# The last pair's second half of values moved into the tail of each batch, with a turning DMA of its own

## The reference

```
x = x + attention(layernorm(x))        16 heads of 64, causal, w_qkv 1024 x 3072, w_out 1024 x 1024
x = x + cross(layernorm(x), ctx)       query/key of ctx (1024 x 512 by 512 x 128), softmax over 1024 x 1024,
                                       the normed x times the attention's transpose
x = x + gated_ffn(layernorm(x))        8 experts, low rank 8, the best expert chosen per token
```

## Time and profile before

| | |
|---|---|
| Time, median of 3 runs | 2646.89 us (2642.32 to 2650.19) |
| The profiled execution | 2647.89 us |
| Its span in the trace | 2646.1 us |
| PE busy | 2395.5 us, 91% of the span |
| DVE, ACT, POOL busy | 69%, 31%, 27% |
| Chain that ended last | PE 59%, DVE 19%, DMA 8%, issue 7% |

### The profile page before, as it was taken

The page is one execution under the profiler, slowest core; times in us unless marked ns, Lnnn a source line. Parts: engine busy times, 40 slices in busy tenths (PEclk is TensorE's granted clock), DMA queues, the critical chain, the costliest instruction groups (busy, mean ns, idle before and its releaser), DMA issues.

```text
span 2646.1 us, 38038 instructions
## 1 busy us (share of the span) xinstructions
PE 2395.5 (91%) x14411; PEld 1175.0 (44%) x14411; DVE 1817.5 (69%) x3457; ACT 816.8 (31%) x1629; POOL 714.9 (27%) x981
## 2 busy tenths in 40 slices
PE   4888998799989999899998999979988999988996
PEld 1334443454544444454453444444444444445444
DVE  6677887657856777656866777765695767675566
ACT  2444333322123333321213333341221333342110
POOL 3332444124202222213412222212430222221220
PEclk9999999899989999999998999989998999999997
DMA  7687888866537767866745777686662676776543
GB/s 213 158 207 167 190 182 176 208 145 148 126 93 151 146 136 148 181 160 149 153 104 124 142 149 141 131 200 158 142 145 86 137 149 143 144 167 163 112 86 90
DMA packets 983131, 393.50 MB, mean 149 GB/s; under 512 B 936796, under 2 KB 946012, under 8 KB 982948
## 3 DMA queue, kind: packets, MB, share of 16 engines
q1 hardware_dynamic: 980356, 381.63, 65.9%
q10 hardware_dynamic: 2592, 9.44, 1.1%
HBM read 122.56 MB, written 33.55 MB: 59 GB/s over the span
## 4 chain that ended last, share of the span: by engine, by line
PE 59%; DVE 19%; DMA 8%; issue 7%; ACT 3%; POOL 3%; SPq 1%; ACTq 0%; POOLq 0%; DVEq 0%
PE ps_p L564 8%; PE ps_p L566 8%; PE ps_p L565 8%; DMA r<-pn 7%; PE ps_s L564 7%; PE ps_s L566 6%; PE ps_s L565 6%; PE ps_s L624 6%; PE ps_o L651 5%; DVE pn L885 5%; DVE peak L925 2%; ACT probs L803 2%; DVE bn L890 2%; PE ps_s L629 1%; POOL pn L1180 1%
## 5 line engine op out<-in xcount | busy, mean ns | idle before, releaser
L1180 POOL TENSOR_SCALAR pn<-probs,rden 128x640 f16<-128x640 f32 (+7 forms) x512 | 396.4, 787 | 1264.4 <-DVE rden L937 760.7
L803 ACT ACTIVATE probs<-ps_s,low,sizes 128x640 f32<-128x640 f32 (+7 forms) x512 | 421.2, 826 | 861.2 <-DVE low L928 750.9
L885 DVE SCALAR_TENSOR_TENSOR pn<-probs,rden,pn 128x640 f16<-128x640 f32 (+7 forms) x512 | 461.3, 937 | 153.9 <-POOL pn L1180 152.4
L564 PE MATMUL ps_p<-r,w 128*128 128x512 f16 x1344 | 515.7, 384 | 3.4 <-DVE qk L885 3.2
L565 PE MATMUL ps_p<-r,w 128*128 128x512 f16 x1344 | 515.1, 383 | 0.0
L566 PE MATMUL ps_p<-r,w 128*128 128x512 f16 x1344 | 514.8, 383 | 0.0
L624 PE MATMUL ps_s<-qk 64*128 64x512 f16 (+3 forms) x2304 | 243.3, 338 | 122.3 <-ACT probs L803 111.7
L925 DVE TENSOR_REDUCE peak<-ps_s 128x2 f32<-128x1280 f32 (+3 forms) x128 | 241.5, 1887 | 89.5 <-PE ps_s L629 86.5
L651 PE MATMUL ps_o<-r,vn 128*64 128x512 f16 (+3 forms) x2304 | 214.1, 343 | 35.4 <-issue 35.2
L624 PEld LDWEIGHTS ps_s<-qk 64*128 64x128 f16 x2304 | 91.6, 96 | 268.9 <-ACT probs L803 146.5
L566 PEld LDWEIGHTS ps_p<-r,w 128*128 128x128 f16 x1344 | 132.5, 99 | 162.2 <-issue 6.1
(11 more groups left out here) (191 smaller groups left out, 3523.5 us busy)
## 6 DMA issues: line engine op xcount, KB each, us to landing
w<-w_pairs SPq DMA_DIRECT2D x72, 512.0 KB, 4.0
r<-wo_pairs SPq DMA_DIRECT2D x16, 1024.0 KB, 6.2
w_raw<-in_x SPq DMA_DIRECT2D x32, 512.0 KB, 4.3
out<-r SPq DMA_DIRECT2D x32, 512.0 KB, 2.9
w_pairs<-w SPq DMA_DIRECT2D x24, 512.0 KB, 7.0
qk<-in_x SPq DMA_DIRECT2D x24, 512.0 KB, 4.5
w_raw<-in_ctx_t SPq DMA_DIRECT2D x16, 512.0 KB, 5.2
w_raw<-in_w_qkv ACTq DMA_DIRECT2D x12, 512.0 KB, 6.3
```

Of the source, the lines that this page charges most:

```text
L564: pe.matmul(ps, lh, rh, start=start and k == ks[0], stop=False)
L803: act.activation(probs_part(q, j, w), ps_s[:, j, scores(q)], ACT.Exp, bias=low[:, n % 2, i:i + 1], scale=sc(n), accum_out=den[:, n % 2, i: ...
L885: dve.scalar_tensor_tensor(out=to, in0=bank, scalar=scale, in1=rounded, op0=ALU.mult, op1=ALU.subtract).then_inc(ok, 1)
L1180: pool.tensor_scalar(to, src, scale, 1.0, ALU.mult, ALU.mult).then_inc(ok, 1)
```

## The change

The four parts P210 to P213 leave the body of pair 6 of each batch and stand in the tail, two ahead of S2 and two ahead of S3. CH21 and CL21 move later in the ACT and DVE lists. `vt16` and `vn` are laid out by halves of the tokens; the last pair's values are turned by two DMAs, V for the first half at the old place in the SP list and V1 after T3. SP's tail opens with T0, and OI0 to OI3 stand behind it. OI0 to OI2 wait only until the part of P21 that reads the same rows is over; KI, KH and KL each wait for their own third of the projections; M0 of the last pair waits for the first half of the values alone.

```
 PE_TAIL
-    S2 S3 M1- S4 G0 S5 G1 M0 S6 G2 B00 S7 ...
+    P210 P211 S2 P212 P213 S3 M1- S4 G0 S5 G1 M0 S6 G2 B00 S7 ...
 DVE_TAIL
-    X0 L70- L71- CL21 R0 X1 L00 L01 X2 R1 L10 ...
+    X0 L70- L71- R0 X1 L00 L01 X2 R1 CL21 L10 ...
 ACT_TAIL
-    E00 E01 CH21 E10 E11 E20 E21 KH JH0 ...
+    E00 E01 E10 E11 E20 E21 CH21 KH JH0 ...
 SP_TAIL
-    OI0 OI1 T0 T1 OI2 T2 OI3 JI2 T3 T4 JI3 T5 ...
+    T0 OI0 OI1 T1 OI2 OI3 T2 JI2 T3 V1 T4 JI3 T5 ...
...
-        vt16 = sb(es, "vt16", [P, 2, SEQ], F16)
-        vn = sb(es, "vn", [P, 2, 2, TB, P], F16)
+        vt16 = sb(es, "vt16", [P, 2, 2, HALF], F16)
+        vn = sb(es, "vn", [P, 2, 2, 2, PARTS, P], F16)
...
+        xt_free = sem("xt_free")
...
+                    if p == PAIRS - 2 and off == 1 and kind == "P" and args[:2] == (2, 1):
+                        continue
...
                     elif kind == "V":
+                        if n % PAIRS < PAIRS - 1:
+                            sp.wait_ge(c_ok, 6 * n + 6)
+                            if n >= 2:
+                                sp.wait_ge(m_ok, 2 * n - 2)
+                            sp.dma_start_transpose(vn[:, n % 2, :, :, :, :].rearrange("p h s k d -> p (h s k) d"),
+                                                   vt16[:, :, :, :].rearrange("p h s d -> p (h s d)")).then_inc(v_in, 16)
+                        else:
+                            h = len(a)
+                            sp.wait_ge(c_ok, 6 * n + 5 + h)
                             sp.wait_ge(m_ok, 2 * n - 2)
+                            sp.dma_start_transpose(vn[:, n % 2, h, :, :, :].rearrange("p s k d -> p (s k) d"),
+                                                   vt16[:, h, :, :].rearrange("p s d -> p (s d)")).then_inc(v_in, 16)
...
                     elif kind == "OI":
-                        sp.wait_ge(part_ok, 6 * PAIRS * (b + 1))
+                        if i < PARTS - 1:
+                            sp.wait_ge(xt_free, 3 * b + i + 1)
+                        else:
+                            sp.wait_ge(part_ok, 6 * PAIRS * (b + 1))
...
                     elif kind == "KI":
-                        sp.wait_ge(part_ok, 6 * PAIRS * (b + 1))
+                        sp.wait_ge(part_ok, 6 * PAIRS * (b + 1) - 4)
...
                         if part == PARTS - 1:
                             mm.then_inc(part_ok, 1)
+                        elif p == PAIRS - 1 and (t, h) == (2, 1):
+                            mm.then_inc(xt_free, 1)
...
-                        pe.wait_ge(v_in, 16 * (n + 1))
+                        pe.wait_ge(v_in, 16 * (n + 1 + b + (g if p == PAIRS - 1 else 0)))
...
                     elif kind == "KH":
                         act.wait_ge(k_in, 16 * (b + 1))
+                        act.wait_ge(part_ok, 6 * PAIRS * (b + 1) - 2)
...
                     elif kind == "KL":
                         dve.wait_ge(kh_ok, b + 1)
+                        dve.wait_ge(part_ok, 6 * PAIRS * (b + 1))
```

More of the change, by code:

```diff
@@ L61 @@
 PE_TAIL = """
-    S2 S3 M1- S4 G0 S5 G1 M0 S6 G2 B00 S7 G3 B01 B10 B11 M1 B20 N0 B21 N1 B30 N2 B31 N3 B40 N4 B41 N5 B50 N6 B51 N7
+    P210 P211 S2 P212 P213 S3 M1- S4 G0 S5 G1 M0 S6 G2 B00 S7 G3 B01 B10 B11 M1 B20 N0 B21 N1 B30 N2 B31 N3 B40 N4 B41 N5 B50 N6 B51 N7
     B60 B61 B70 B71 Z00 Z01 Z10 Z11 Z20 Z21 F0 Z30 Z31 F1 D0 Z40 Z41 F2 D1 U0 Z50 Z51 F3 D2 U1 Z60 Z61 F4 D3 U2
@@ L67 @@
 DVE_TAIL = """
-    X0 L70- L71- CL21 R0 X1 L00 L01 X2 R1 L10 L11 R2 X3 KL JL0 R3 OL1- X4 L20 L21 QL0 JL1 R4 L30 L31 X5 L40
+    X0 L70- L71- R0 X1 L00 L01 X2 R1 CL21 L10 L11 R2 X3 KL JL0 R3 OL1- X4 L20 L21 QL0 JL1 R4 L30 L31 X5 L40
     L41 QL1 JL2 R5 OL0 X6 L50 L51 R6 QL2 JL3 X7 L60 L61 R7 QL3 RA0 L70 L71 RA1 LB0 OL1 CX0 LL0 LB1 CR0 RA2 CX1 CLO0
@@ L77 @@
 ACT_TAIL = """
-    E00 E01 CH21 E10 E11 E20 E21 KH JH0 E30 E31 OH1- QH0 JH1 E40 E41 E50 E51 QH1 JH2 OH0 E60 E61 QH2 JH3 E70 E71
+    E00 E01 E10 E11 E20 E21 CH21 KH JH0 E30 E31 OH1- QH0 JH1 E40 E41 E50 E51 QH1 JH2 OH0 E60 E61 QH2 JH3 E70 E71
     QH3 LX0 OH1 CE0 LX1 CE1 CE2 CE3 LX2 CE4 CE5 CE6 CE7 AX0+ AX1+ AX2+ TX0 LX3 AX3+ TX1
@@ L89 @@
 SP_TAIL = """
-    OI0 OI1 T0 T1 OI2 T2 OI3 JI2 T3 T4 JI3 T5 RI0 T6 RI1 T7 WD0+ WD1+ WD2+ RI2 RI3 CT0 LT0 CT1 RI4
+    T0 OI0 OI1 T1 OI2 OI3 T2 JI2 T3 V1 T4 JI3 T5 RI0 T6 RI1 T7 WD0+ WD1+ WD2+ RI2 RI3 CT0 LT0 CT1 RI4
     LT1 RI5 CT2 CT3 RI6 CT4 CT5 RI7 CT6 CT7 AI0+ AI1+ AI2+ AT0+ AT1+ AI3+ LT2 AT2+
@@ L208, in decoder_layer @@
         c_probs = qk16[1][:, :].bitcast(F32).rearrange("p (s d) -> p s d", s=2)
-        vt16 = sb(es, "vt16", [P, 2, SEQ], F16)
-        vn = sb(es, "vn", [P, 2, 2, TB, P], F16)
-        xh3 = vn[:, 1, :, :, :].rearrange("p s k d -> p s (k d)")
+        vt16 = sb(es, "vt16", [P, 2, 2, HALF], F16)
+        vn = sb(es, "vn", [P, 2, 2, 2, PARTS, P], F16)
+        xh3 = vn[:, 1, :, :, :, :].rearrange("p h s k d -> p h (s k d)")
         probs0 = sb(es, "probs0", [P, 2 * SEQ])
@@ L456, in attend @@
                     elif kind == "V":
-                        sp.wait_ge(c_ok, 6 * n + 6)
-                        if n >= 2:
+                        if n % PAIRS < PAIRS - 1:
[7 more added lines that the diff above has]
+                            sp.wait_ge(c_ok, 6 * n + 5 + h)
                             sp.wait_ge(m_ok, 2 * n - 2)
-                        sp.dma_start_transpose(vn[:, n % 2, :, :, :].rearrange("p s k d -> p (s k) d"),
-                                               vt16[:, :, :].rearrange("p s d -> p (s d)")).then_inc(v_in, 16)
+                            sp.dma_start_transpose(vn[:, n % 2, h, :, :, :].rearrange("p s k d -> p (s k) d"),
+                                                   vt16[:, h, :, :].rearrange("p s d -> p (s d)")).then_inc(v_in, 16)
                 def constants():
@@ L650, in attend @@
                                 for j in range(2):
-                                    mm = pe.matmul(ps_o[rows(j), g, c:HALF], vn[:, n % 2, vs, kb, rows(j)],
+                                    mm = pe.matmul(ps_o[rows(j), g, c:HALF], vn[:, n % 2, kb // PARTS, vs, kb % PARTS, rows(j)],
                                                    keys_of(g, j, s, kb), start=kb == 0 and vs == 0 and s == 0,
@@ L774, in attend @@
                             if n > 0:
-                                act.wait_ge(v_in, 16 * n)
-                            to = vt16[:, 0, half(h)]
+                                act.wait_ge(v_in, 16 * (n + n // PAIRS))
+                            to = vt16[:, h, 0, :]
                         act.activation(to, proj_bank(n, t, h), ACT.Copy, scale=Q_OUT).then_inc(ch_ok, 1)
@@ L913, in attend @@
                         else:
-                            hi, lo = (vt16[:, s, half(h)] for s in range(2))
+                            hi, lo = (vt16[:, h, s, :] for s in range(2))
                         pair_rest(lo, proj_bank(n, t, h), Q_OUT, hi, c_ok)
```

## The result

The changed kernel takes 2651.89 us (median of 7 runs, 2648.05 to 2654.91) against 2645.27 for the kernel before (7 runs, 2641.78 to 2650.19): ratio 1.0026, 95% interval 1.0016 to 1.0036. It is slower, by 4 to 10 us; the forecast was 14. The way was right and the size twice too large. The measured time lies in the forecast's range, 2650 to 2676, only because its lower end had been put there for the warm M1-; on its own the forecast had 2655 to 2676.

A forecast was written before the change was run, and what follows sets the result against it. PE, busy nine tenths of the span, was the bound, with T7's and T3's landings setting the tails. Head - 2.6, gap + 13.8 and clock + 3.0 made + 14.2 us on 2646.9: 2661 us, range 2650 to 2676.

The forecast's parts named there:

- warm M1-: Rival: denser PE work in the head brings M1- to full clock, 8.6 us gained, 2652 us; chance 0.12.
- The order of SP: Tails: T0 holds SP until M1- ends, all four OI loads then precede T3, so M0 starts later; 13.8 us lost.
- the gap: From M1-'s end to M0's start, over four tails: forecast 86.4 us against 72.6 before, 13.8 us lost.
- E: The end of M1- in a tail; forecast T1's landing near E + 10 and M0 at E + 21.6.
- small gaps: Allowance of 0.5 us per tail added to the byte sum up to T3's landing, giving M0 at E + 21.6.
- M1- left as it is: M1- in the tails keeps its time, since it still waits 3 to 4 us and the clock falls there; 0.
- The clock at M0: M0 and S6 run slow in all four tails after a hole of about 7 us; 3.0 us lost.
- The head: Ahead of M1-: X0, L71 and T7's issue come 0.6 us earlier, KI moves out of T7's way; 2.6 us gained.
- Hidden loads: Rival: transposes pass beside loads or faster than 208 GB/s, M0 stays, only the head counts; 2644 us, chance 0.07.
- loads and transposes pass at one rate: The page's rate in the DMA queue, counted inside the hidden-loads rival; chance 0.03 of its 0.07.
- PE work decides: Rival: PE's own work bounds the tail, so 5.2 us of projections are saved in each, 20.8 us; 2626, chance 0.05.
- Stalls: Rival: T1 and T2 behind loads each lose up to 1.9 us, 15 us more, 2676; with the forecast, chance 0.74.

The follow-up runs named there:

- e2: The kernel before with SP's new order alone (T0 ahead of OI0 and OI1, OI2 and OI3 behind T1): 2662.88 us, ratio 1.0054.
- e4: The kernel before with OI3 moved behind T3 and JI2 behind T2, projections and values as before: 2630.22 us, ratio 0.9941.
- e5: The kernel before with 8 useless matmuls behind S3, inside the wait ahead of M1-: ratio 1.0.
- e10: The kernel before with SP's new order and 8 useless matmuls ahead of M1-: ratio 1.0032.
- e7: The changed kernel with OI0, OI1 ahead of T0, OI3 behind T3, 8 useless matmuls ahead of M1- and 14 between G0 and S5: 2624.89 us, 0.9916.
- e9: The changed kernel with OI0, OI1 ahead of T0, OI3 behind T2, and one V for the last pair instead of two: ratio 1.0005.
- e6: The changed kernel, its SP order too, with 8 useless matmuls ahead of M1- and 20 ahead of M0: 2652.23 us, ratio 1.0015.
- e1: The changed kernel with OI0 and OI1 ahead of T0 again and OI3 behind T2: 2640.26 us, ratio 0.997.
- e3: The changed kernel with OI0 and OI1 ahead of T0, JI2 behind T2 and OI3 behind T3: 2627.43 us, ratio 0.9928.

## Why the prediction was right in its way and wrong in its size

**The order of SP.** Right, and the largest term. Forecast + 13.8 us for the gap, measured + 11.3 in the changed kernel and + 10.4 in e2. T1's landing (E + 10.8 for E + 10), the idle DMA engines during M1- and M0 on T3's landing came as written. The size is too large by the 0.5 us that I added to each tail for small gaps: without it the sum gives M0 at E + 21.1, and the four tails measured 21.8, 20.6, 21.1 and 20.4, on average 21.0. In the second tail the DMA engines are busy for 0.97 of the time from M1- to M0, so there are few gaps to pay for; in the kernel before T2 and T3 were issued only as L2 and L3 ended (1121.54 and 1126.68 us), which is where its gaps may lie.

**M1- left as it is.** This is the term that failed. The prediction took it at 0, with a rival of 8.6 us at a chance of 0.12; it measured - 5.4 us (26.2 to 20.8). The step behind the 0 was that the clock falls in the wait of 3 to 4 us just ahead of M1-, which the change leaves there. Two things in it were wrong. The waits of before weren't all of that length: the earlier trace rows have 1.94, 4.02, 3.44 and 2.73 us, and M1- took 7.12 us behind the shortest. And the clock hadn't fallen in the wait. PE in the two waits of tails one and two, the kernel before first (the third number from the end is the granted clock):

```profile
469.50:471.40 1.90, 0.01 (x1) 0.50 1.06 240
1105.60:1109.50 3.90, 0.00 (x0) 0.50 1.18 179
```

```profile
471.75:474.00 2.25, 0.00 (x0) 1.00 1.08 232
1104.60:1108.60 4.00, 0.01 (x1) 0.96 1.19 243
```

Before, the clock was at 0.50 through the whole wait: it had gone by then, with S3, behind the hole of 3.50 us. In the changed kernel PE is dense from S0 to S3 and the clock stands at 1.00 and 0.96 in the same wait. So in tail one M1- runs at full rate from its start; in tail two it starts at 0.50 and is back at 1.00 from 1112 us on, half way (5.92 us). So what loses the clock ahead of M1- is the hole ahead of S3, which the moved projections fill. That they do it, the table shows (0 of 12 tails with M1- at 4.41 us in before, e2 and e4, 13 of 20 with them moved). e5 and e10 show that useless matmuls bring the clock back too, if not always: M1- took 4.41 to 4.86 us in their eight tails, and in e7, with the same fill on top of the moved projections, 5.98 in one of four.

What it is worth depends on the order: nothing in the old one (e5, e9); in the new, most of it by the changed kernel against e2 (M1- 5.3 us less, gap 0.9 more), about half by e10 against e2 (M1- 8.5 us less, tails 4.5 less). So it mattered here because the same edit that made the loads wait for M1- made its length count. How much of it comes through isn't settled, as e6 shows. The rival's time, 2652 us, is near what was measured, but in part by luck: M1- gave 5.4 us and not 8.6, and the gap cost 2.5 less than forecast.

**The clock at M0.** Forecast + 3.0 for M0 and S6, measured + 1.8 in M0 and 0.1 in the rest. M0 was at half rate in all four tails as said; the slow stretch didn't reach far beyond.

**The head.** Forecast - 2.6, measured - 1.4, and not by the route that I gave. X0 did start earlier, as its row shows against the earlier trace rows, but T7 was issued at the same distance from S7 (12.88 us in both, 1101.11 - 1088.23 and 1101.32 - 1088.44). Between them DVE lost it again:

```profile
1097.11 0.28 DVE L940 TENSOR_REDUCE peak<-ps_s 128x1 f32<-128x128 f32 x1
1097.31 0.28 DVE L941 TENSOR_REDUCE peak<-ps_s 128x1 f32<-128x128 f32 x1
1097.62 1.09 DVE L947 TENSOR_SCALAR low<-peak,sizes 128x2 f32<-128x2 f32 x1
1098.62 2.47 DVE L904 SCALAR_TENSOR_TENSOR pn<-probs,rden,pn 128x1024 f16<-128x1024 f32 x2
```

The third row is where: `low` took 1.09 us and ended as POOL's H7 ended (last section), and it ended with H7 in the kernel before too. So an earlier X0 couldn't bring T7 forward. What was gained came from T7's landing, 7.4 us after issue in this tail instead of 8.2, with KI out of its way; in the same tail H1 starts 7.0 to 7.6 us after T7's issue in e1, e3, e6 and e9, and 8.3 to 8.9 in e2, e4, e5 and e10. That KI is the cause was not tried alone.

**The sum.** - 1.4 - 5.4 + 11.3 + 1.8 + 0.1 = 6.4 us (6.5 before rounding), against 6.9 by the ratio and 14.2 forecast. Of the 7.8 us missed (14.2 - 6.4), 5.4 are M1-, 2.5 the gap, 1.1 the clock at M0, and the head takes back 1.2.

**The other rivals.** Hidden loads: excluded by the gap. That loads and transposes pass at one rate, to which 0.03 of the chances went, no run shows: loads passed at 402 GB/s and transposes at 208. PE work decides: excluded, PE waits ahead of M1- and of M0 in every tail. Stalls: T1 behind OI1 landed within 0.8 us of its time; none seen.

## What to carry to other kernels

Where one queue issues everything, an entry that waits holds all behind it: before loads are moved behind such an entry, add up the bytes that will then stand between it and the transfer that the bottleneck waits for, and put behind that transfer whatever is needed later (here one load, OI3, in four tails: 11 us from e1 to e3, 16 us in the kernel before). A shorter step is worth something only if what ends the next wait starts from its end, so price it together with the order of issue and not by itself. And when a rearrangement fills idle time ahead of a waiting block, cost the block at both clock levels, and read in which hole the granted clock falls: here it was the one before, and that was the largest error.

## What the runs showed of the hardware

A two-column operation on DVE, L947 above, took 1.09 us where it took 0.36 in the kernel before. It ended at 1098.71 us, just as two POOL instructions ended that had started at 1096.47 and run for 2.21 us:

```profile
1096.47 2.21 POOL L1200 TENSOR_SCALAR pn<-probs,rden 128x1024 f16<-128x1024 f32 x2 [7.47 <-DVE rden L956]
```

In the kernel before the same operation ended with POOL too, at 1098.91 for 1098.89; there it started later and so looked short:

```profile
1098.55 0.36 DVE L928 TENSOR_SCALAR low<-peak,sizes 128x2 f32<-128x2 f32 x1
1096.68 2.21 POOL L1180 TENSOR_SCALAR pn<-probs,rden 128x1024 f16<-128x1024 f32 x2 [7.47 <-DVE rden L937]
```

The same holds in the other three tails of both kernels (1.07 to 1.09 us, or 0.36 and 0.37 where it started late), and most of these operations in the kernel take 0.23. It looks as if it had waited for POOL. The Trainium skill (GPSIMD Engine Reference, section Specifications) has the two engines share their SBUF interfaces for some DVE instructions; the trace is in line with it, and no run here tried it by itself.

PE's clock, in the second tail unless said: a wait of 4.0 us after a dense stretch was followed by a M1- of 5.92 us, the same wait after a stretch with a 3.5 us hole by one of 7.21. In tails one and four waits of 2.3 and 2.1 us after a dense stretch were followed by 4.41, and in the kernel before waits of 1.9 and 2.7 us by 7.12 and 5.75. With 8 matmuls inside the wait M1- was at 4.41 in all four tails of e10.

Transposes passed at 208 GB/s and large loads at 402. In the new order the landings fit transfers that pass one behind the other in their order of issue: T1 landed at E + 10.8 where that gave about E + 10, behind two loads issued just ahead of it, while T0, with nothing ahead, landed in 2.4 us; and M0 came at E + 21.0 on average for E + 21.1.
